# A selective-scan stage on one Trainium2 core: Softplus as one ScalarE function, a 1024-column w·B step, and pair sums added by TensorE

## The reference, cut to what matters

```python
xz = h @ w_in
xc, z = xz[:, :D_INNER], xz[:, D_INNER:]
u = silu(causal_conv4(xc) + conv_b)
dbc = u @ w_xp
dt = softplus(dbc[:, :DT_RANK] @ w_dt + b_dt)
B, C = dbc[:, DT_RANK:DT_RANK + D_STATE], dbc[:, DT_RANK + D_STATE:]
dA = exp(dt[:, :, None] * A[None])            # A = -exp(A_log)
dBu = dt[:, :, None] * B[:, None, :] * u[:, :, None]
hst = dA[t] * hst + dBu[t]                    # for each t in turn
y = (hst @ C[t]) + u * D_skip
out = (y * silu(z)) @ w_out
```

## Time and profile before

| | |
|---|---|
| median of three runs | 2748.58 us (2747.08 to 2750.45) |
| the profiled execution's own time | 2750.08 us |
| its span | 2748.1 us |
| mean granted clock of TensorE | 0.94 of full speed |
| busy: TensorE, VectorE, ScalarE, GpSimd | 84%, 81%, 38%, 36% of the span |

### The profile page before, as it was taken

One profiled execution on the slowest core, in us unless ns is written; L12 is line 12 of the kernel. 1 busy time (PEld: TensorE's weight loads), 2 busy tenths in 40 slices (PEclk: granted clock), 3 DMA queues, 4 the chain that ended last, 5 costly groups with the idle time before them and its releaser, 6 DMA issues.

```text
span 2748.1 us, 22503 instructions
## 1 busy us (share of the span) xinstructions
PE 2307.8 (84%) x6968; PEld 1294.8 (47%) x6968; DVE 2213.9 (81%) x2409; ACT 1033.1 (38%) x1745; POOL 977.4 (36%) x409
## 2 busy tenths in 40 slices
PE   0347788999999999999999888888888988886776
PEld 0222344444458888888874344433333444333333
DVE  5889888877627666656542999999999999999997
ACT  0000000000015555555433555555555555555552
POOL 0000000000000000000000778778777787777554
PEclk9968799999999999999999999999999999997888
DMA  8999999889756555555556555555555564541111
GB/s 337 383 402 410 394 394 381 365 351 369 275 222 238 214 192 217 218 187 202 195 212 256 203 192 194 190 191 195 194 188 213 184 214 177 191 171 69 61 63 58
DMA packets 108326, 643.03 MB, mean 234 GB/s; under 512 B 14224, under 2 KB 15024, under 8 KB 42672
## 3 DMA queue, kind: packets, MB, share of 16 engines
q1 hardware_dynamic: 92160, 604.02, 57.7%
q10 hardware_dynamic: 16048, 37.57, 3.9%
HBM read 625.28 MB, written 16.25 MB: 233 GB/s over the span
## 4 chain that ended last, share of the span: by engine, by line
PE 49%; DVE 34%; issue 13%; ACT 2%; ACTq 1%; DMA 1%; POOL 0%; DVEq 0%; POOLq 0%
PE ps L853 20%; PE ps L771 12%; DVE arena L568 12%; DVE arena L686 7%; PE ps L893 6%; DVE ps L672 5%; PE ps L972 4%; PE ps L934 3%; DVE ring L686 2%; PE ps L793 2%; DVE arena L693 1%; ACTq L1002 1%; DVE arena L731 1%; DVE parts L718 1%; PE ps L914 1%
## 5 line engine op out<-in xcount | busy, mean ns | idle before, releaser
L460 POOL TENSOR_TENSOR rstd<-base,minus_half 128x8 f32<-128x8 f32 (+1 forms) x40 | 85.8, 2144 | 1492.2 <-DVE base L508 924.9
L853 PE MATMUL ps<-adj_parts,h_parts 128*128 128x512 f32 x2592 | 593.6, 390 | 2.5 <-ACT adj_parts L1068 2.1
L893 PE MATMUL ps<-ring,diag_h 128*128 128x512 f32 x1152 | 542.6, 604 | 2.1 <-DVE arena L658 2.0
L476 POOL TENSOR_TENSOR arena<-arena 128x1024 f32<-128x1024 f32 x192 | 461.4, 2409 | 230.7 <-ACT state L1135 229.7
L853 PEld LDWEIGHTS ps<-adj_parts,h_parts 128*128 128x128 f32 x2592 | 484.7, 188 | 108.8 <-ACT adj_parts L1068 4.6
L568 DVE TENSOR_TENSOR arena<-arena,ring 128x2048 f32<-128x2048 f32 x208 | 476.8, 2292 | 64.0 <-DMA ring<-adj 45.8
L771 PE MATMUL ps<-ring,arena 128*128 128x512 f32 x928 | 432.0, 626 | 64.0 <-DMA ring<-adj 64.0
L686 DVE TENSOR_TENSOR_SCAN arena<-arena,state,ps 128x512 f32<-128x512 f32 x384 | 469.4, 1264 | 1.0 <-ACT arena L1143 0.5
L1143 ACT ACTIVATE arena<-arena,a_sb 128x512 f32<-128x512 f32 x512 | 338.6, 709 | 61.7 <-DVE arena L733 61.2
L672 DVE TENSOR_TENSOR ps<-arena,ps 128x512 f32<-128x512 f32 x512 | 327.6, 685 | 19.0 <-PE ps L914 18.0
L893 PEld LDWEIGHTS ps<-ring,diag_h 128*128 128x128 f32 x1152 | 222.6, 196 | 253.2 <-issue 250.1
(11 more groups left out here) (94 smaller groups left out, 1950.6 us busy)
## 6 DMA issues: line engine op xcount, KB each, us to landing
ring<-adj SPq DMA_DIRECT2D x480, 1024.0 KB, 6.5
arena<-c_scratch SPq DMA_DIRECT2D x128, 512.0 KB, 3.8
diag_h<-adj SPq DMA_DIRECT2D x32, 1024.0 KB, 12.2
arena<-x ACTq DMA_DIRECT2D x16, 512.0 KB, 5.1
x_scratch<-arena ACTq DMA_DIRECT2D x8, 512.0 KB, 3.0
arena<-x_scratch ACTq DMA_DIRECT2D x16, 256.0 KB, 4.5
out<-arena ACTq DMA_DIRECT2D x16, 256.0 KB, 3.9
lower_scratch<-arena ACTq DMA_DIRECT2D x7, 512.0 KB, 2.6
```

What stands on the lines that cost most here:

```text
L476: nc.gpsimd.tensor_tensor(buf, buf, c_row, ALU.mult).then_inc(mult_done, 1)
L853: last = nc.tensor.matmul(acc[:, c, :], h_parts[:, blk % 2, layer, h_part, a * F:(a + 1) * F], adj_parts[:, buf, adj_part, c * MM:(c + 1) ...
L893: last = nc.tensor.matmul((acc_c if i else y_ps)[:, c, :], tile_of(h1, JT * s + a), blk[:, a * STRIP + c * MM:a * STRIP + (c + 1) * MM], s ...
```

## The change

Softplus: the dt products are copied from PSUM (with their bias) straight into dt's buffer, and one ScalarE activation, Softplus, 128 × 1024, runs on it in place. The four ScalarE functions and VectorE's three steps go, and the stage TIME_STEP with them; the second dt product moves from slot 12 to slot 13, in the slot's order behind the gcn product, and is copied there. w·B: one VectorE step of 1024 columns writes two banks; B rows lie in banks 6 and 4, and the step writes banks 5 and 6 in even slots, 5 and 4 in odd ones. Pair sums: the 26 sums of two pairs by VectorE go, and TensorE adds every pair to y_ps by a product with the identity, in every even slot. Left out of the diff below are declarations of semaphores and a wait on `dt_ready` that is no longer needed in front of the copy to `cv`.

```diff
@@ -66,13 +66,11 @@
 
 GCN, BIAS, STATS, POWER, NORMALISE = -19, -19, -17, -17, -15
 TRANSPOSE, XZ, SILU, DBC, SPLIT = -13, -12, -7, -6, -5
-DT, SOFTPLUS, TIME_STEP, WEIGHTED_U = -4, -3, -2, -1
+DT, SOFTPLUS, WEIGHTED_U = -4, -3, -1
 NSUM = 6
 LOAD_X1, SKIP, GATE, OUT, RESIDUAL = 12, 20, 21, 25, 25
 
 
-QUADS = (1, 3)
-QUAD = 6
 SPARED = 3
 
 F32 = mybir.dt.float32
@@ -172,7 +170,8 @@
     misc = []
     for g in range(FIRST_SLOT, LAST_SLOT):
         for stage, kinds in ((GCN, ["gcn"]), (OUT, ["out"]), (TRANSPOSE, ["tr"]), (XZ, ["xz0"]), (XZ + 1, ["xz1"]),
-                             (XZ + 2, ["xz2"]), (XZ + 3, ["xz3"]), (DBC, ["dbc"]), (DT, ["dt0", "dt1"])):
+                             (XZ + 2, ["xz2"]), (XZ + 3, ["xz3"]), (DBC, ["dbc"]), (DT, ["dt0"]),
+                             (DT + 1, ["dt1"])):
             k = chunk_at(g, stage)
             if k is not None:
                 misc += [(kind, k) for kind in kinds]
@@ -275,9 +274,9 @@
         ps_w = ps[:, 6:8, :]
         acc_c = ps[:, 2:4, :]
         y_ps = ps[:, 0:2, :]
-        b_ps = [ps[:, 4, :], ps[:, 5, :]]
-        first_dbu_ps = ps[:, 6, :]
         misc_ps = ps[:, 7, :]
+        b_ps = [ps[:, 6, :], ps[:, 4, :]]
+        dbu_ps = [ps[:, 5:7, :], ps[:, 5:3:-1, :]]
 
         weights_in = sem("weights_in")
         ring_in = [sem(f"ring_in{i}") for i in range(RING)]
...
@@ -366,20 +361,7 @@
 
             eng.wait_ge(misc_free, misc_at[kind, k] + 1)
 
-        def dbu_of(g, h):
-            return b_ps[g % 2] if h else first_dbu_ps
-
         PAIRS_ADDED = (NCH - SPARED) * (DS // 2)
-
-        def added_to_next(G):
-
-            return G % (DS // 2) in QUADS and G < PAIRS_ADDED
-
-        def quads_before(G):
-            return sum(added_to_next(g) for g in range(G))
-
-        def nsums_before(G):
-            return G - quads_before(G)
 
         weight_loads = [
             (ident[:, :], ident_in), (w0t_sb[:, :], w0t), (b0_sb[:, :], b0.to_broadcast([P, F])),
@@ -663,34 +645,24 @@
                 if 0 <= g < NCH * DS:
                     k, n = divmod(g, DS)
                     if n == 0:
-                        dve.wait_ge(dt_ready, 2 * (k + 1))
+                        dve.wait_ge(w_ready, k + 1)
                     dve.wait_ge(b_ready, g + 1)
-                    for h in range(HALVES):
-                        if g and h == 0:
-
-                            dve.wait_ge(scan_done, 2 * g - 1)
-                        nc.vector.tensor_tensor(dbu_of(g, h), w[k % 2][:, h, :], b_ps[g % 2], ALU.mult)\
-                            .then_inc(dbu_done, 1)
+                    if g:
+
+                        dve.wait_ge(scan_done, 2 * g - 1)
+                    nc.vector.tensor_tensor(dbu_ps[g % 2], w[k % 2],
+                                            b_ps[g % 2].unsqueeze(1).to_broadcast([P, HALVES, T]), ALU.mult)\
+                        .then_inc(dbu_done, 1)
                     dve.wait_ge(da_ready, g + 1)
                     if k:
                         dve.wait_ge(state_saved, g - DS + 1)
                     if g >= HSB:
 
-                        G = (g - HSB) // 2
-                        if added_to_next(G):
-                            dve.wait_ge(quad_done, quads_before(G + 1))
-                        else:
-                            dve.wait_ge(nsum_done, nsums_before(G + 1))
+                        dve.wait_ge(nsum_done, (g - HSB) // 2 + 1)
+                    dve.wait_ge(dbu_done, g + 1)
                     for h in range(HALVES):
-                        dve.wait_ge(dbu_done, 2 * g + 1 + h)
-                        nc.vector.tensor_tensor_scan(hs[g % HSB][:, h, :], da[g % 2][:, h, :], dbu_of(g, h),
+                        nc.vector.tensor_tensor_scan(hs[g % HSB][:, h, :], da[g % 2][:, h, :], dbu_ps[g % 2][:, h, :],
                                                      state[:, h, n:n + 1], ALU.mult, ALU.add).then_inc(scan_done, 1)
-
-                G, odd = divmod(g - QUAD, 2)
-                if not odd and 0 <= G < NCH * DS // 2 and added_to_next(G):
-                    dve.wait_ge(pair_done, G + 2)
-                    both = hs[(2 * G + 2) % HSB]
-                    nc.vector.tensor_tensor(both, both, hs[2 * G % HSB], ALU.add).then_inc(quad_done, 1)
 
                 k = chunk_at(g, BIAS)
                 if k is not None:
@@ -719,26 +691,14 @@
                         .then_inc(parts_ready, 1)
 
 
-                k = chunk_at(g, SOFTPLUS)
-                if k is not None:
-                    ex, w1 = w[k % 2], dt[k % 2]
-                    dve.wait_ge(ex_ready, k + 1)
-                    nc.vector.scalar_tensor_tensor(ex, w1, -1.0, ex, ALU.add, ALU.subtract).then_inc(w1_ready, 1)
-                k = chunk_at(g, TIME_STEP)
-                if k is not None:
-                    ex, w1 = w[k % 2], dt[k % 2]
-                    dve.wait_ge(w1_ready, k + 1)
-                    step(nc.vector.scalar_tensor_tensor(ex, cv, 0.0, ex, ALU.max, ALU.subtract))
-                    dve.wait_ge(log_ready, k + 1)
-                    nc.vector.tensor_tensor(w1, ex, w1, ALU.add).then_inc(dt_ready, 1)
                 k = chunk_at(g, WEIGHTED_U)
                 if k is not None:
-                    dve.wait_ge(dt_ready, 2 * k + 1)
+                    dve.wait_ge(dt_ready, k + 1)
                     dve.wait_ge(u_ready, k + 1)
-                    nc.vector.tensor_tensor(w[k % 2], dt[k % 2], u[k % 2], ALU.mult).then_inc(dt_ready, 1)
+                    nc.vector.tensor_tensor(w[k % 2], dt[k % 2], u[k % 2], ALU.mult).then_inc(w_ready, 1)
                 k = chunk_at(g, SKIP)
                 if k is not None:
-                    dve.wait_ge(nsum_done, nsums_before(DS // 2 * (k + 1)))
+                    dve.wait_ge(nsum_done, DS // 2 * (k + 1))
                     if k:
                         dve.wait_ge(misc_full, misc_at["out", k - 1] + 1)
                     for h in range(HALVES):
@@ -917,24 +877,20 @@
                 if not odd and 0 <= G < NCH * DS // 2:
 
                     pair = G % (DS // 2)
-                    if not added_to_next(G):
-                        terms = [hs[2 * G % HSB]]
-                        if G >= PAIRS_ADDED:
-                            pe.wait_ge(mult_done, 2 * G + 2)
-                            terms.append(hs[(2 * G + 1) % HSB])
-                        elif pair and added_to_next(G - 1):
-                            pe.wait_ge(quad_done, quads_before(G))
-                        else:
-                            pe.wait_ge(pair_done, G + 1)
-                        first = all(added_to_next(g) for g in range(G - pair, G))
-                        if first and G >= DS // 2:
-                            pe.wait_ge(y_free, G // (DS // 2))
-                        for j, term in enumerate(terms):
-                            for h in range(HALVES):
-                                last = nc.tensor.matmul(y_ps[:, h, :], ident[:, :], term[:, h, :],
-                                                        start=first and j == 0,
-                                                        stop=pair == DS // 2 - 1 and j == len(terms) - 1)
-                        last.then_inc(nsum_done, 1)
+                    terms = [hs[2 * G % HSB]]
+                    if G < PAIRS_ADDED:
+                        pe.wait_ge(pair_done, G + 1)
+                    else:
+                        pe.wait_ge(mult_done, 2 * G + 2)
+                        terms.append(hs[(2 * G + 1) % HSB])
+                    if pair == 0 and G:
+                        pe.wait_ge(y_free, G // (DS // 2))
+                    for j, term in enumerate(terms):
+                        for h in range(HALVES):
+                            last = nc.tensor.matmul(y_ps[:, h, :], ident[:, :], term[:, h, :],
+                                                    start=pair == 0 and j == 0,
+                                                    stop=pair == DS // 2 - 1 and j == len(terms) - 1)
+                    last.then_inc(nsum_done, 1)
                 k = chunk_at(g, GCN)
                 if k is not None:
                     pe.wait_ge(s1_ready, k // CPS + 1)
@@ -984,9 +940,9 @@
                         last = nc.tensor.matmul(m_ps[0:KD, :], wx_sb[:, h, :], u[k % 2][:, h, :],
                                                 start=h == 0, stop=h == HALVES - 1)
                     last.then_inc(misc_full, 1)
-                k = chunk_at(g, DT)
-                if k is not None:
-                    for h in range(HALVES):
+                for h in range(HALVES):
+                    k = chunk_at(g, DT + h)
+                    if k is not None:
                         pe.wait_ge(wdt_ready, 1)
                         pe.wait_ge(parts_ready, k + 1)
                         m_ps = use_misc((f"dt{h}", k))
...
@@ -1203,22 +1158,16 @@
                     nc.scalar.activation(parts[k % 2][:, :], bcv[0:KD, :], ACT.Copy).then_inc(bc_high, 1)
```

(51 more changed lines are left out.)

## The result

The changed kernel takes **2686.6 us** (median of four runs, 2683.1 to 2688.9), against 2749.5 for the kernel before on the same chip: ratio 0.977, 95% interval 0.975 to 0.979. The forecast was 2670, with a range from 2642 to 2702. The direction and the range held; of the 81 us forecast 63 came.

What follows compares the result with a forecast made beforehand. VectorE was taken to set the second half's pace, TensorE 11 us behind. Terms summed to 81.2 us gained, 70 of it in chunks 0 to 12: 2750.1 to 2668.9, rounded up to 2670 us; range 2642 to 2702.

Steps and rivals of the forecast that it cites:

- Slots 0 to 3: Start of a chunk: nothing but four wide w·B steps, 0.3 us lost.
- Slots 4 to 9: Slot 4 to the residual of slot 9: TensorE, with slot 8's pair sum added, is late; 0.5 us lost a chunk.
- Residual to BIAS, and BIAS to slot 14: Slot 9's residual to slot 14: VectorE loses the second add, 1.7 us gained; L726 goes, 1.1 gained a chunk.
- Slot 14: Main term: without L731 and L733 the slot falls from 8.80 to 3.63 us, 5.2 gained a chunk.
- Slot 15: Scan 15 waits 1.7 us for ScalarE's chain of 7.15 us from BIAS's start; with the wide step, 1.8 lost.
- Sum: All terms of one chunk together: 5.4 us gained.
- A start that waits for an end comes 0.03 to 0.04 behind it: Scan after the wide w·B step: step to scan 1.27 us in place of 1.20, 0.07 lost a slot.
- TensorE as the bound: Rival, slots 4 to 13: another 2 us a chunk lost to TensorE, giving 2696 us; chance 0.17.
- The wait in slot 15 isn't there: Rival: both table loads leave ScalarE's chain, 24 us more gained, 2646 (2637 with a step of 1.21); chance 0.12.
- a switch of 2.7 us: Rival: ScalarE empties its pipe round a table load, 2.8 us more in 13 chunks, 2706; chance 0.05.
- The slower one: Rival: the wide w·B step is dear, at 2.03 us losing 0.8 in each of 256 slots, 2874; chance 0.04.
- The change does less than it says: Rival, slots 4 to 13: moving the adds to full TensorE gives no net gain; partly in the forecast; no own chance.

Runs made afterwards that it cites:

- the run with the wait first: The changed kernel with the scan's wait for the wide w·B step written ahead of its other waits: 2674.6 us, ratio 0.972.
- the run with dt1 first: The changed kernel with the second dt product ahead of the gcn product, its copy and Softplus ahead of Relu: 2655.3 us, ratio 0.965.
- one step later: The changed kernel with dt1 ahead of the gcn product and the w·B step in two 512-column halves: 2634.5 us, ratio 0.957.
- the halves: The changed kernel with the w·B step back in two halves of 512 columns, on the new banks: 2670.2 us, ratio 0.970.
- Softplus alone: The changed kernel with w·B in halves and the sums of two pairs back on VectorE: 2688.7 us, ratio 0.977.
- dt1 first with halves and one or two adds: The changed kernel with dt1 ahead of gcn, w·B in halves, and VectorE adding slot 8's pair sum alone (2624.9 us) or both (2646.9 us).
- vector adds: The changed kernel with the 26 sums of two pairs back on VectorE, their products off TensorE: 2702.4 us, ratio 0.981.
- the single add: The changed kernel with dt1 ahead of gcn, w·B in halves and only slot 8's pair sum back on VectorE: 2624.9 us, ratio 0.955.

## Why the prediction was right, and where its sizes were off

The mechanism was right: VectorE was the bound, slot 14 was the main term, and the three places named as late next, the residual of slot 9, scan 15 and the shared bank in slot 13, are the three waits of the trace after. Not every sign came as named: slot 14 takes 3.9 and not 3.6, the step-to-scan time is 1.34 and not 1.27, the scan's wait in chunk 11 is 1.40 and not 1.5 to 2, and seven of the chunks 1 to 12 are above 74 us, which the forecast had as a sign of being wrong. The steps, with the slots of the table (chunks 1 to 12) against the forecast's chunk:

- *Slots 0 to 3*: 0.3 lost, as forecast, though by chance. The wide step costs 0.16 a bare slot, not 0.07, and slot 1 takes 0.18 less than before: a step of 128 × 4 in it (L512 before, L494 after) takes 0.48 and not 0.83, since it starts nearer to the end of the GpSimd product beside it and ends 0.02 behind that in both kernels. The forecast had no such term.
- *Slots 4 to 9*: 27.8 to 28.3, 0.5 lost, as forecast.
- *Residual to BIAS, and BIAS to slot 14*: 1.7 + 1.1 forecast; slots 10 to 13 went from 19.4 to 17.3, 2.1. Missing are four gaps of 0.10 and the 0.4 by which SPLIT (L718 before, L690 after) grew, from 1.34 to 1.76 on average.
- *Slot 14*: 5.2 forecast, 4.9 measured. Of the difference 0.1 is the gap again; the rest is the B row of slot 15, late in six of the twelve chunks (by 0.44 in chunk 11), where TensorE stood behind BIAS.
- *Slot 15*: 1.8 lost forecast, 2.3 measured. The wait itself was a little smaller than the 1.7 forecast (18.1 us in 12 scans, 1.5 each): the copy of dt1 came 0.3 late, since dt1 took 0.77 us behind the pause, at the lower clock, and not 0.47, but VectorE came later too. The 0.7 that the forecast put at nothing is the small step L490, 0.17 before and 0.81 on average after, which now meets a product of GpSimd.
- *Sum*: 5.4 forecast, **3.8 measured** by the medians. By their whole length chunks 1 to 12 gave 48.2 us of 64.8, 16.6 short. Chunks 0, 13 and 14 gave 6.4, 3.9 and 5.3 (forecast 5.4, 3.5, 5.2), and the start 4.9 (3.6: from BIAS on it was 3.6, and BIAS came 1.3 sooner, which the forecast hadn't counted). The slots and the start together thus gave 67.8 of 81, 13 short; in the profiled execution another 5 were lost in the first half, which the change doesn't touch, so that part of the miss is no error of the sum.

**The step that failed** is thus no mechanism but the terms of slots 10 to 15, for three reasons. "A start that waits for an end comes 0.03 to 0.04 behind it" was read from a pair in which the wait rides on the waiting instruction. The scan has four waits, and the forecast didn't ask which of them is carried where; the run with the wait first measured what that cost, 12 us. And dt1 was counted to follow "beside Relu" at TensorE's full clock, though the same paragraph had TensorE stand still in front of it. Third, VectorE's other steps were taken over at their old lengths, though GpSimd's products beside them were to move: the small step of slot 15 cost 0.7 a chunk and SPLIT 0.4.

The rivals: TensorE as the bound had 0.17 and gave 2696, nearer to the measured 2686.6 than the forecast's 2670, but not the reason: B rows ended VectorE's idle time for only 21.1 us in all, under the 40 that were named as its sign, and the run with dt1 first took 31 us off with TensorE's work as it was. It comes closer one step later: at about 70 us a chunk TensorE is busy for 67, and VectorE waits for it at the residual and at B rows (19.8 and 16.2 us in all between 1600 and 2550). That it is the bound there is not shown, since taking both pair sums from it made the kernel 12 us slower. "The wait in slot 15 isn't there" is out, the two loads stand in the rows. The third, a switch of 2.7 us, is out too: Softplus starts 0.01 behind the load of 1.28 and the copy ends 0.02 ahead of it; the Trainium skill (ScalarE: Activation LUTs, What ACT_TABLE_LOAD costs) adds a drain of 1380 ns for each switch, and none shows here, nor where a function of 1.06 us stands right in front of the load (0.02 between them). The slower one is out as to its price, for the wide step takes 1.22 us, but it had the right part of the change: that part loses.

"The change does less than it says" had the pair sums as a small gain, 1.2 a chunk; the runs have them at 0.9 a chunk and 15.8 us in all beside the wide step, and 18.5 us beside the halves.

Why SPLIT takes 1.34 us on average in the kernels with an add in slot 8 and halves (before, Softplus alone, dt1 first with halves and one or two adds), 0.97 with vector adds and 1.7 to 2.1 in those without an add, for the same work, the traces answer. In each of the chunks 0 to 12 of all 13 traces it took 0.69 us where no product of GpSimd ran as it started, and otherwise it ended 0.55 behind the end of that product. In chunk 11 before, the product had 0.70 to run, and SPLIT took 1.25; after, 1.11 and 1.66; with halves, 1.46 and 2.01. So a change that moves VectorE by a few tenths of a microsecond against GpSimd changes the length of such a step by as much, with no reason in the step itself. In the last comparison it is 0.8 us of each chunk, more than half of what the single add gained. What a run with GpSimd out of the way would take in all is open.

## What to carry to other kernels

When two engines work nearly as much as each other, price a saved instruction by the stretch it stands in, not by its length: 5.2 us of slot 14 came through almost whole, and the 1.5 us add of slot 8 was worth less than nothing. A moved product also takes its place in every queue and every shared buffer that it passes: dt1 behind the gcn product in the one PSUM bank cost 31 us, half of what the change won. A wider instruction is no saving if the next one can then no longer start under it, and the order in which an instruction's waits are written can cost more than the width did (12.0 us and 4.4). And where VectorE and GpSimd work side by side, a step's length in the trace before is no constant: look where the product beside it will end.

## What the runs showed of the hardware

- A wait written first rides on the waiting instruction, and it starts 0.03 us behind the end it waits for; one of several, written last, becomes an instruction of its own and makes it 0.13.
- TensorE after a pause of 2.3 us: four records of 512 columns in 3.18 us and not 1.88, and a 512-column fp32r product in 0.77 and not 0.47, with the granted clock at 0.72 over those 6.2 us. With the pause at 0.87 the clock stayed at 1.00.
- One ScalarE function on 128 × 1024 took 1.06 us whether it was Silu, Ln or Softplus, with a load in front; the load was 1.28 each time, 0.02 behind the instruction in front of it where that was just done, and with no drain beside it.
- Some VectorE steps that read SBUF ended with the GpSimd product that ran as they started. One with two SBUF inputs, 40 × 512, took 0.69 us alone and otherwise ended 0.55 us behind the product (up to 2.88 us long); steps of 128 × 4 took 0.14 and 0.17 us alone and otherwise ended 0.02 to 0.03 behind it (once 0.11; up to 1.4 us long). The w·B step of 1024 columns, with one input in SBUF and one in PSUM, took 1.20 to 1.23 us in all 256 slots of the changed kernel, 83 of them wholly beside such a product.
